# MLP down products of layers 1 and 2 in plain fp32, and the key and value projections of the last layer folded into other weights

## The chip, the cores and the metric

The kernel runs on one core of a Trainium2 chip. The metric is the device time of one execution in microseconds. The time before is the median of three runs.

## What is computed

Four different transformer layers run one after the other on x of 64 batches x 128 tokens x 128 channels, with a condition vector and a context of 77 tokens per batch. Layer 0 has windowed attention, top-k cross attention and a SwiGLU MLP; layers 1 and 2 have self attention, cross attention and a GELU MLP; the last one mixes the context in and routes each token over three experts. The change touches the GELU MLP of layers 1 and 2 and the last layer:

```python
# layers 1 and 2, MLP (512 hidden channels)
x_norm2 = modulate(_ln(x), shift_m, scale_m)
h = gelu(x_norm2 @ W_mlp1 + b_mlp1)
x = x + gate_m[:, None] * (h @ W_mlp2 + b_mlp2)
# last layer
nx = layer_norm(x, gamma, beta)
q = nx @ Wq;  k = context @ Wk;  v = context @ Wv
weights = softmax(q @ k.T * H ** -0.5)
evidence = weights @ v
combined = concatenate([nx, evidence, anchor], axis=-1)
router_probs = softmax(combined @ router_W + router_b)
h = silu(combined @ e_w1 + e_b1)          # three experts, 256 hidden channels each
routed = sum((h @ e_w2 + e_b2) * router_probs)
g = sigmoid(silu(combined @ gate_w1 + gate_b1) @ gate_w2 + gate_b2)
x + g * (routed @ out_w + out_b)
```

## The kernel before

x stays in SBUF from the first load to the last store (`x_res`). Each stage is a block with a list of instructions per engine, written by hand, and the engines are tied by counting semaphores; a list is worked through in order, and the stages follow each other with a barrier. All stages work on groups of G = 4 batches, 16 groups, so that a matmul has 4 x 128 = 512 columns, one PSUM bank.

A product in the MLPs and for the up products of the last layer is made of three fp32r matmuls (`product3`, L236 to L240): weights and input are each split into a high part (a cast to fp32r) and a low part (the value minus the high part), and low x high, high x low and high x high are summed in PSUM. Other products are plain fp32 matmuls.

`mlp_phase` (L1775) is used for three layers. For layers 1 and 2 (`swiglu` false) a group runs so: DVE takes the statistics of x (`ln_stats`, `ln_variance`), POOL takes the power -0.5 (`rstd_of`), DVE normalises (`ln_apply`, L1895), PE transposes (L2008), ACT modulates into `hT`, DVE splits `hT` in two (`split_h`, L1902 and L1904). Then for each of NC = 4 chunks of 128 hidden channels: PE makes the up product into one of four banks `u_ps`; ACT applies GELU into `hid` (L1993); DVE casts the high part (L1943); POOL subtracts for the low part (L1870), in the fourth chunk DVE does (L1949); PE makes the down product into `y_ps`, LD = 3 chunks behind the up product. ACT then applies the gate (`apply_gate`, L1970), PE transposes back (L2048), and DVE adds to x (L1924). The lists work on neighbouring groups at once: in the body of group g, PE transposes `xn` of group g + 1 after the first chunk and `pg` of group g - 2 in the second, DVE has x of g - 2, the statistics of g + 2 and `split_h` of g + 1 in its list. PE's list of the down product waits for the low part:

```python
pe.wait_ge(s_lo, n + 1)
product3(nc, y_ps[:, par, :], parts(w2, c * C), [hid2[:, c, k, :] for k in range(2)],
         start=(c == 0), stop=(c == NC - 1)).then_inc(s_down, 1)
```

`refine_phase` (L2057) is the last layer. For iteration i its PE list has the seven up products of group i (`up`, two banks `u_ps`, each product six fp32r matmuls: three on the normalised x, three on the evidence), and between them the small steps of groups i + 1 and i + 2: transposed attention weights and evidence of i + 1 (L2511, L2518), transposes of `xn` of i + 2 (L2481), the router of i + 1 (L2528, L2530), then key, query and value projections of i + 2 (L2486, L2491, L2496) through one bank `l_ps`, and the scores (L2503); at its end the gate (L2581) and the down products of i (L2593). The three projections follow each other through `l_ps`: ACT copies the keys out, then the queries, and DVE the values, and the next projection waits for the copy before. ACT evacuates each up product with four SiLU (L2420). Before group 0, `prepare` multiplies weights with each other (e2 with the output matrix, the anchor parts) once the weights have landed, and ACT and POOL split the up weights `w1s`.

## Time and profile before

| | us |
|---|---|
| median of three runs | 3493.57 |
| lowest, highest run | 3489.97, 3500.9 |
| profiled execution, its time | 3496.01 |
| profiled execution, its span | 3494.2 |
| PE busy | 3048.8 (87%) |
| PE weight loads | 2051.7 (59%) |
| DVE busy | 2754.6 (79%) |
| ACT busy | 2253.2 (64%) |
| POOL busy | 1170.7 (34%) |
| mean granted TensorE clock | 0.947 |

The span is the time from the first to the last instruction of the profiled execution; its time also has what lies around that. Busy shares are means over stages with different limits. In the order of the program: layer 0's attentions end near 1240 us; its MLP follows until about 1430; layer 1's attentions until 2097, its MLP until 2247; layer 2's attentions until 2934, its MLP until 3084; then the last layer to the end. A duration of a matmul is longer than the distance to the next one, as matmuls overlap; lengths are best read from start to start. The granted clock is 1.00 at 2.4 GHz and 0.50 at 1.2 GHz.

### The profile page before, as it was taken

The numbers are of one execution on the slowest core, as the hardware profiler recorded it, in microseconds if no ns is written. First come the engines' busy times: TensorE is split into PE (matmuls) and PEld (weight loads), VectorE is DVE, ScalarE is ACT, GpSimd is POOL, SyncE is SP. The second block draws the span as 40 slices with busy tenths as digits, with TensorE's granted clock in tenths as the row PEclk, the third lists the DMA queues.
The fourth block names the chain that finished last, engine by engine and source line by source line (L and its number), as shares of the span: only waits on it lengthen the run. The fifth ranks groups of instructions, "written<-read, shape, count | busy, mean of one in ns | idle before, by whom it ended". The sixth has DMA issues, their size and how long they took to land. (4 is left out here: it accounts for less than half of the span.)

```text
span 3494.2 us, 94730 instructions
## 1 busy us (share of the span) xinstructions
PE 3048.8 (87%) x32127; PEld 2051.7 (59%) x32127; DVE 2754.6 (79%) x12477; ACT 2253.2 (64%) x5572; POOL 1170.7 (34%) x1374
## 2 busy tenths in 40 slices
PE   6999967777777779799999997789999997879999
PEld 3444434444444457566666665556666665568887
DVE  4878779999999978588877759778887776946665
ACT  2666667777777667377766665457776665646665
POOL 0000046666666656311122215521112212532111
PEclk9999979999899889799999999989999999979999
DMA  1111000000000000244444420034444440000000
GB/s 47 44 49 37 14 12 7 9 9 9 8 9 7 3 1 1 72 106 107 107 103 100 104 60 1 20 97 108 106 107 101 105 100 17 1 24 13 11 12 16
DMA packets 139908, 162.90 MB, mean 47 GB/s; under 512 B 41318, under 2 KB 88870, under 8 KB 139174
## 3 DMA queue, kind: packets, MB, share of 16 engines
q1 hardware_dynamic: 127270, 130.80, 14.9%
q0 software_dynamic: 12160, 26.04, 3.2%
q8 instruction: 262, 4.29, 0.5%
q14 instruction: 216, 1.77, 0.2%
HBM read 16.33 MB, written 4.19 MB: 6 GB/s over the span
## 5 line engine op out<-in xcount | busy, mean ns | idle before, releaser
L1374 ACT ACTIVATE attn_pT<-attn_t 128x512 f32<-128x512 f32 (+1 forms) x1024 | 555.7, 597 | 319.7 <-PE attn_t L1631 319.5
L1491 DVE TENSOR_REDUCE attn_mx<-attn_s 128x4 f32<-128x512 f32 (+1 forms) x1024 | 549.4, 578 | 140.2 <-PE attn_s L1616 139.1
L1616 PEld LDWEIGHTS attn_s<-packed_keys,packed_queries 32*128 32x128 f32 x4096 | 276.7, 189 | 161.5 <-DVE attn_mx L1491 96.0
L659 ACT ACTIVATE topk_prob<-topk_s,topk_nmx 128x77 f32<-128x77 f32 x1024 | 248.3, 326 | 181.7 <-DVE topk_work L840 156.0
L1289 POOL DMA_DIRECT2D packed_queries<-attn_om x256 | 142.7, 557 | 645.0 <-ACT attn_om L1367 640.9
L1616 PE MATMUL attn_s<-packed_keys,packed_queries 32*128 32x128 f32 (+1 forms) x4096 | 341.5, 287 | 13.3 <-DVE attn_mx L1491 7.2
L503 POOL TENSOR_SCALAR topk_mask<-topk_work 128x308 f32<-128x308 f32 x256 | 250.1, 977 | 238.9 <-DVE topk_work L845 237.8
L1023 PE MATMUL topk_s<-kbd,topk_qT 128*128 128x308 f32 x512 | 215.4, 505 | 129.7 <-ACT topk_prob L659 129.2
L1656 PE MATMUL attn_o<-attn_pT,attn_vp 128*18 128x128 f32 (+1 forms) x8192 | 326.3, 277 | 0.0
L1631 PE MATMUL attn_t<-packed_queries,packed_keys 32*128 32x128 f32 (+1 forms) x4096 | 299.8, 264 | 0.0
L1870 POOL TENSOR_TENSOR mlp_hid<-mlp_hid 128x512 fp32r<-128x512 f32 x160 | 210.1, 1314 | 156.8 <-DVE mlp_hid L1943 107.9
L1631 PEld LDWEIGHTS attn_t<-packed_queries,packed_keys 32*128 32x128 f32 (+1 forms) x4096 | 227.4, 166 | 4.7 <-ACT attn_pT L1374 3.4
L1676 PE MATMUL attn_l<-packed_keys 128*128 128x512 f32 x636 | 225.2, 444 | 0.7 <-DVE attn_vp L1481 0.7
L507 POOL TENSOR_TENSOR topk_prob<-topk_prob,topk_mask 128x308 f32<-128x308 f32 x256 | 213.8, 835 | 21.3
L840 DVE MATCH_REPLACE8 topk_work<-topk_top,topk_s 128x77 f32<-128x77 f32 x1024 | 220.2, 223 | 0.0
L1656 PEld LDWEIGHTS attn_o<-attn_pT,attn_vp 128*18 128x18 f32 (+1 forms) x8192 | 181.3, 97 | 60.6 <-issue 44.4
L845 DVE MATCH_REPLACE8 topk_work<-topk_top,topk_work 128x77 f32<-128x77 f32 x1024 | 215.3, 219 | 0.0
L1023 PEld LDWEIGHTS topk_s<-kbd,topk_qT 128*128 128x128 f32 x512 | 86.6, 210 | 195.5 <-ACT topk_prob L659 141.4
L1033 PEld LDWEIGHTS topk_t<-ident,topk_prob 128*77 128x77 f32 x1024 | 146.5, 163 | 58.2 <-issue 16.5
L829 DVE MAX8 topk_top<-topk_s 128x8 f32<-128x77 f32 x1024 | 167.0, 222 | 15.4 <-PE topk_s L1023 15.0
L1033 PE MATMUL topk_t<-ident,topk_prob 128*77 128x128 f32 x1024 | 170.4, 294 | 1.8 <-POOL topk_prob L507 1.8
L1285 POOL TENSOR_TENSOR attn_rstd<-attn_vareps,neg_half 128x4 f32<-128x4 f32 x64 | 65.8, 1029 | 299.9 <-DVE attn_vareps L1449 299.8
(316 smaller groups left out, 7869.7 us busy)
## 6 DMA issues: line engine op xcount, KB each, us to landing
packed_queries<-attn_qT SPq DMA_DIRECT2D x720, 64.0 KB, 2.2
packed_keys<-attn_kT SPq DMA_DIRECT2D x384, 64.0 KB, 2.1
packed_queries<-attn_om POOLq DMA_DIRECT2D x256, 64.0 KB, 2.3
packed_queries<-zero_rows SPq DMA_DIRECT2D x120, 128.0 KB, 2.7
packed_keys<-attn_kT SPq DMA_DIRECT2D x384, 39.0 KB, 2.2
kbd<-window_kT SPq DMA_DIRECT2D x512, 8.0 KB
kbd<-topk_kT SPq DMA_DIRECT2D x512, 4.8 KB
x_res<-in_x SPq DMA_DIRECT2D x16, 192.0 KB, 2.6
```

Source lines behind the costliest of these rows:

```text
L503: nc.gpsimd.tensor_scalar(mask[:, u % 2, :], work[:, n % NP, :], NEG / 2, None, ALU.is_le).then_inc(s_mask, 1)
L659: last = nc.scalar.activation(prob[:, n % NP, h * keys:(h + 1) * keys], s_ps[:, u % 2, h * keys:(h + 1) * keys], ACT.Exp, scale=SCALE, bia ...
L840: last = nc.vector.match_replace(wk_[now][:, h, :], top[:, u % 2, h, :], sc[:, h, :], NEG)
L845: last = nc.vector.match_replace(wk_[past][:, h, :], top2[:, c % 2, h, :], wk_[past][:, h, :], NEG)
L1023: last = nc.tensor.matmul(s_ps[:, u % 2, 0:cols], qT[:, par, b * T:(b + 1) * T], r.kbd[:, HU * g:HU * g + HU, b * keys:(b + 1) * keys], st ...
L1033: last = nc.tensor.transpose(t_ps[0:rows, c % 2, j * T:(j + 1) * T], prob[:, n % NP, j * rows:(j + 1) * rows], r.ident[:, :])
L1374: nc.scalar.activation(pT[0:keys, c % 2, h, :], t_ps[0:keys, h, :], ACT.Exp, scale=SCALE).then_inc(s_exp, 1)
L1491: nc.vector.tensor_reduce(mx[:, (c // 2) % 2, 2 * k + h, :], sc, AX.X, ALU.max).then_inc(s_max, 1)
L1616: last = nc.tensor.matmul(s_ps[:, h, k * KW:(k + 1) * KW], r.qp[32 * j:32 * j + 32, buf, k, b * T:(b + 1) * T], r.kp[32 * j:32 * j + 32, b ...
L1631: last = nc.tensor.matmul(t_ps[0:keys, h, k * T:(k + 1) * T], r.kp[32 * j:32 * j + 32, buf, k, b * KW:b * KW + keys], r.qp[32 * j:32 * j + ...
L1656: last = nc.tensor.matmul(o_ps[32 * k:32 * k + 18, v * T:(v + 1) * T], vp[0:keys, buf, b, k, v, a, :], pT[0:keys, c % 2, a, k * T:(k + 1) ...
L1676: nc.tensor.matmul(l_ps[:, :], r.kp[:, buf, 0, 0:T], r.kp[:, buf, 0, :], start=True, stop=True)
```

## The change

In the MLP of layers 1 and 2, the hidden values and the down weights are no longer split. A down product is one fp32 matmul of `hid` with the weights as they lie in SBUF; it waits for GELU alone, and GELU waits for the down product that read the same buffer. DVE's cast and DVE's or POOL's subtraction go, and the split of the down weights ahead of the first group. Layer 0's MLP stays as it is, with three fp32r matmuls.

In the last layer the host hands over Wq, Wk and Wv transposed. The kernel multiplies Wq by the transpose of Wk once (`wqk`), projects the queries with that, and takes the scores against the raw context. The evidence becomes the weights' mean of the raw context, which is loaded by DMA from SP's queue, four batches a time, into three buffers; Wv is multiplied once into the parts of the expert, gate and router weights that the evidence meets (`folded`, `wr`), in `prepare`. ACT takes the high parts of these from PSUM, DVE the low parts. The key and value projections of every group go, with ACT's copy of the keys and DVE's copy of the values.

```diff
-        w1, w2 = sb("w1", [C, 2, W1], F32R), sb("w2", [C, 2, NC * C], F32R)
+
+        w1 = sb("w1", [C, 2, W1], F32R)
+        w2 = sb("w2", [C, 2, NC * C], F32R) if swiglu else None
...
-                    if swiglu or c < NC - 1:
+                    if swiglu:
...
-                split_weights(nc, nc.vector.tensor_copy, dve, w2, r.W(name, 0, NC * C), s_w, 2)
+                if swiglu:
+                    split_weights(nc, nc.vector.tensor_copy, dve, w2, r.W(name, 0, NC * C), s_w, 2)
...
-                    if not swiglu:
-                        after(dve, s_down, n - 3)
-                        dve.wait_ge(s_hid, n + 1)
-                        nc.vector.tensor_copy(hid2[:, c, 0, :], hid[:, c % NB, :]).then_inc(s_hi, 1)
                     if c == 2 and nxt2:
                         ln_apply(g + 2)
-                    if c == 3 and not swiglu:
-                        dve.wait_ge(s_hi, n + 1)
-                        after(dve, s_lo, n)
-                        nc.vector.tensor_tensor(hid2[:, c, 1, :], hid[:, c % NB, :], hid2[:, c, 0, :].bitcast(F32),
-                                                ALU.subtract).then_inc(s_lo, 1)
...
-                        after(act, s_lo, n - 3)
+                        after(act, s_down, n - 3)
...
-                    pe.wait_ge(s_w, 4)
+                    if swiglu:
+                        pe.wait_ge(s_w, 4)
+                if not swiglu:
+                    pe.wait_ge(s_hid, n + 1)
+                    nc.tensor.matmul(y_ps[:, par, :], r.W(name, c * C), hid[:, c % NB, :],
+                                     start=(c == 0), stop=(c == NC - 1)).then_inc(s_down, 1)
+                    return
                 pe.wait_ge(s_lo, n + 1)
                 product3(nc, y_ps[:, par, :], parts(w2, c * C), [hid2[:, c, k, :] for k in range(2)],
                          start=(c == 0), stop=(c == NC - 1)).then_inc(s_down, 1)
...
-        qT, kT, v = sb("qT", [C, GT]), sb("kT", [C, K4]), sb("v", [S, G, C])
+        qT, v = sb("qT", [C, GT]), sb("v", [S, 3, G, C])
...
+        def folded():
+
+            yield t_ps[:, :].rearrange("c (e n) -> c e n", e=2), [up_part(p, 1)[:, 0:2] for p in range(2)]
+            yield u_ps[:, 1:2, 2 * C:2 * C + RH], [up_part(p, 1)[:, 2:3] for p in range(2)]
+            yield g_ps[:, B * E:B * E + C], [w1s[:, p, E * 2 * RH + C:NU] for p in range(2)]
...
+            def load_values(g):
+                sp.dma_start(v[:, g % 3], r.ctx_v[:, G * g:G * g + G, :]).then_inc(s_vin[g % 3], 16)
...
+            for g in range(3):
+                load_values(g)
             for g in range(NG):
                 p = g % 2
+                if there(g + 3):
+                    sp.wait_ge(s_eps, g + 1)
+                    load_values(g + 3)
...
-                nc.gpsimd.tensor_tensor(w1s[:, 1, 0:E * 2 * RH].rearrange("c (e n) -> c e n", e=E), e1_parts,
-                                        w1s[:, 0, 0:E * 2 * RH].bitcast(F32).rearrange("c (e n) -> c e n", e=E),
-                                        ALU.subtract).then_inc(s_w1lo, 1)
-                nc.gpsimd.tensor_tensor(w1s[:, 1, E * 2 * RH:NU], r.W("g1", 0, 2 * C),
-                                        w1s[:, 0, E * 2 * RH:NU].bitcast(F32), ALU.subtract).then_inc(s_w1lo, 1)
+                nc.gpsimd.tensor_tensor(up_part(1, 0), e1_first, up_part(0, 0).bitcast(F32), ALU.subtract
+                                        ).then_inc(s_w1lo, 1)
+                nc.gpsimd.tensor_tensor(w1s[:, 1, E * 2 * RH:E * 2 * RH + C], r.W("g1", 0, C),
+                                        w1s[:, 0, E * 2 * RH:E * 2 * RH + C].bitcast(F32), ALU.subtract
+                                        ).then_inc(s_w1lo, 1)
...
-            def values_out(g):
-                dve.wait_ge(s_vps, g + 1)
-                nc.vector.tensor_copy(v[:, :, :], l_ps[0:S, :].rearrange("p (b c) -> p b c", b=G)
-                                      ).then_inc(s_v, 1)
...
+                for k, (product, parts) in enumerate(folded()):
+                    dve.wait_ge(s_fhi, k + 1)
+                    nc.vector.tensor_tensor(parts[1], product, parts[0].bitcast(F32), ALU.subtract).then_inc(s_flo, 1)
...
-            def keys_out(g):
-                act.wait_ge(s_kps, g + 1)
-                nc.scalar.copy(kT[:, :], l_ps[:, 0:K4]).then_inc(s_kT, 1)
...
+                for k, (product, parts) in enumerate(folded()):
+                    if k == 2:
+                        act.wait_ge(s_arb, 1)
+                        nc.scalar.copy(wr[:, :], g_ps[:, B * E + C:B * E + C + E]).then_inc(s_wr, 1)
+                    nc.scalar.copy(parts[0], product).then_inc(s_fhi, 1)
+
+            act.wait_ge(s_qkps, 1)
+            nc.scalar.copy(wqk[:, :], t_ps[:, 0:C]).then_inc(s_wqk, 1)
...
-                after(pe, s_v, g)
+                after(pe, s_qT, g)
                 pe.wait_ge(s_xn, g + 1)
                 for b in range(G):
                     last = nc.tensor.transpose(l_ps[:, b * T:(b + 1) * T], xn[:, b, :], r.ident[:, :])
                 last.then_inc(s_xT, 1)
 
-            def project_keys(g):
+            def project_queries(g):
                 pe.wait_ge(s_nx, g + 1)
-                nc.tensor.matmul(l_ps[:, 0:K4], r.W("k3"), r.ctxT[:, G * g:G * g + G, :], start=True, stop=True
-                                 ).then_inc(s_kps, 1)
-
-            def project_queries(g):
-                pe.wait_ge(s_kT, g + 1)
-                nc.tensor.matmul(l_ps[:, :], r.W("q3"), nx[:, g % NXB, :], start=True, stop=True).then_inc(s_qps, 1)
-
-            def project_values(g):
+                if g == 0:
+                    pe.wait_ge(s_wqk, 1)
+                nc.tensor.matmul(l_ps[:, :], wqk[:, :], nx[:, g % NXB, :], start=True, stop=True).then_inc(s_qps, 1)
+
+            def scores(g):
+                after(pe, s_dif, g)
                 pe.wait_ge(s_qT, g + 1)
                 for b in range(G):
-                    last = nc.tensor.matmul(l_ps[0:S, b * C:(b + 1) * C], r.ctxT[:, G * g + b, :], r.W("v3"),
-                                            start=True, stop=True)
-                last.then_inc(s_vps, 1)
-
-            def scores(g):
-                after(pe, s_dif, g)
-                for b in range(G):
                     last = nc.tensor.matmul(s_ps[:, b * S:(b + 1) * S], qT[:, b * T:(b + 1) * T],
-                                            kT[:, b * S:(b + 1) * S], start=True, stop=True)
+                                            r.ctxT[:, G * g + b, :], start=True, stop=True)
...
-                pe.wait_ge(s_v, g + 1)
+                pe.wait_ge(s_vin[g % 3], 16 * (g // 3) + 16)
                 pe.wait_ge(s_pT, g + 1)
                 for b in range(G):
-                    last = nc.tensor.matmul(t_ps[:, b * T:(b + 1) * T], v[:, b, :], pT[:, b * T:(b + 1) * T],
+                    last = nc.tensor.matmul(t_ps[:, b * T:(b + 1) * T], v[:, g % 3, b, :], pT[:, b * T:(b + 1) * T],
                                             start=True, stop=True)
...
-                                            r.W("rw", E, E), start=False, stop=True)
+                                            wr[:, :], start=False, stop=True)
...
+                pe.wait_ge(s_wqk, 1)
+                for e in range(E):
+                    out = t_ps[:, e * RH:(e + 1) * RH] if e < 2 else u_ps[:, 1, 2 * C:2 * C + RH]
+                    nc.tensor.matmul(out, r.W("v3"), r.W("e1", (e * 3 + 1) * RH, RH), start=True, stop=True)
+                nc.tensor.matmul(g_ps[:, B * E:B * E + C], r.W("v3"), r.W("g1", C), start=True, stop=True)
+                nc.tensor.matmul(g_ps[:, B * E + C:B * E + C + E], r.W("v3"), r.W("rw", E, E), start=True, stop=True)
                 for k in range(2 * E):
...
+            nc.tensor.matmul(t_ps[:, 0:C], r.W("q3"), r.W("k3"), start=True, stop=True).then_inc(s_qkps, 1)
...
-        "q3": a(L3 + "Wq"), "k3": a(L3 + "Wk"), "v3": a(L3 + "Wv"), "rw": rows(a(L3 + "router_W")),
+        "q3": a(L3 + "Wq").T, "k3": a(L3 + "Wk").T, "v3": a(L3 + "Wv").T, "rw": rows(a(L3 + "router_W")),
```

What this does to the lists. On DVE in an MLP of layer 1 or 2, one group's worth before (`mlp_hid` is the hidden tile, `mlp_hT` the modulated input, `mlp_xn` the normalised x):

```order
L1949 TENSOR_TENSOR mlp_hid<-mlp_hid 128x512
L1879 BN_STATS mlp_stats<-x_res 128x6 x4
L1943 CAST mlp_hid<-mlp_hid 128x512
L1924 TENSOR_TENSOR x_res<-mlp_r,x_res 128x512
L1886 BN_AGGR mlp_mv<-mlp_stats 128x2 x4
L1889 TENSOR_SCALAR mlp_vareps<-mlp_mv 128x4
L1943 CAST mlp_hid<-mlp_hid 128x512
L1902 CAST mlp_hT<-mlp_hT 128x512
L1904 TENSOR_TENSOR mlp_hT<-mlp_hT 128x512
L1943 CAST mlp_hid<-mlp_hid 128x512
L1895 TENSOR_SCALAR mlp_xn<-x_res,mlp_mv,mlp_rstd 128x128 x4
```

and of the change:

```order
L1881 BN_STATS mlp_stats<-x_res 128x6 x4
L1927 TENSOR_TENSOR x_res<-mlp_r,x_res 128x512
L1888 BN_AGGR mlp_mv<-mlp_stats 128x2 x4
L1891 TENSOR_SCALAR mlp_vareps<-mlp_mv 128x4
L1904 CAST mlp_hT<-mlp_hT 128x512
L1906 TENSOR_TENSOR mlp_hT<-mlp_hT 128x512
L1897 TENSOR_SCALAR mlp_xn<-x_res,mlp_mv,mlp_rstd 128x128 x4
```

The four casts of `mlp_hid` and its subtraction are gone from between the others, which keep their order.

On PE in the same stage, from the down product before the transposes of `xn` to the next but one, before:

```order
L238 MATMUL mlp_y<-mlp_hid,mlp_w 128x512
L239 MATMUL mlp_y<-mlp_hid,mlp_w 128x512
L240 MATMUL mlp_y<-mlp_hid,mlp_w 128x512
L2008 MATMUL mlp_l<-ident,mlp_xn 128x128 x4
L238 MATMUL mlp_u<-mlp_hT,mlp_w 128x512
L239 MATMUL mlp_u<-mlp_hT,mlp_w 128x512
L240 MATMUL mlp_u<-mlp_hT,mlp_w 128x512
L238 MATMUL mlp_y<-mlp_hid,mlp_w 128x512
L239 MATMUL mlp_y<-mlp_hid,mlp_w 128x512
L240 MATMUL mlp_y<-mlp_hid,mlp_w 128x512
L2048 MATMUL mlp_r<-ident,mlp_pg 128x128 x4
```

and of the change, where L2002 is the L2008 of before:

```order
L2029 MATMUL mlp_y<-mlp_hid,weights 128x512
L2002 MATMUL mlp_l<-ident,mlp_xn 128x128 x4
L238 MATMUL mlp_u<-mlp_hT,mlp_w 128x512
L239 MATMUL mlp_u<-mlp_hT,mlp_w 128x512
L240 MATMUL mlp_u<-mlp_hT,mlp_w 128x512
L2029 MATMUL mlp_y<-mlp_hid,weights 128x512
L2048 MATMUL mlp_r<-ident,mlp_pg 128x128 x4
```

Each three matmuls into `mlp_y` have become one that reads `mlp_hid` and the resident weights.

On PE in the last layer, from the end of the router of group i + 1 to the scores of i + 2, before (six matmuls into `refine_u` are one up product):

```order
L2530 MATMUL refine_g<-weights,refine_ev 128x3
L2486 MATMUL refine_l<-ctxT,weights 128x308
L238 MATMUL refine_u<-refine_nxs,refine_w1s 128x512
...
L240 MATMUL refine_u<-refine_evs,refine_w1s 128x512
L2491 MATMUL refine_l<-refine_nx,weights 128x512
L238 MATMUL refine_u<-refine_nxs,refine_w1s 128x512
...
L240 MATMUL refine_u<-refine_evs,refine_w1s 128x512
L2496 MATMUL refine_l<-weights,ctxT 77x128 x4
L238 MATMUL refine_u<-refine_nxs,refine_w1s 128x512
...
L240 MATMUL refine_u<-refine_evs,refine_w1s 128x512
L2503 MATMUL refine_s<-refine_kT,refine_qT 128x77 x4
```

and of the change:

```order
L2544 MATMUL refine_g<-refine_wr,refine_ev 128x3
L238 MATMUL refine_u<-refine_nxs,refine_w1s 128x512
...
L240 MATMUL refine_u<-refine_evs,refine_w1s 128x512
L2507 MATMUL refine_l<-refine_nx,refine_wqk 128x512
L238 MATMUL refine_u<-refine_nxs,refine_w1s 128x512
...
L240 MATMUL refine_u<-refine_evs,refine_w1s 128x512
L238 MATMUL refine_u<-refine_nxs,refine_w1s 128x512
...
L240 MATMUL refine_u<-refine_evs,refine_w1s 128x512
L2513 MATMUL refine_s<-ctxT,refine_qT 128x77 x4
```

The keys (L2486) and values (L2496) are gone, the queries have moved from L2491 to L2507 with `refine_wqk`, and the scores read `ctxT`.

## Rows read from the trace of the kernel before

**Rows 1.** The core's span and granted clock.

```profile
core 0: 3494.2 us, clock 0.947
```

**Rows 2.** Windows: us, busy PE PEld DVE ACT POOL, clock, DMA share, GB/s.

```profile
2112.40:2238.00 125.60, 103.26 (x466) 74.04 (x465) 115.25 (x290) 79.75 (x172) 72.99 (x58) 1.00 0.00 1
...
3128.80:3437.00 308.20, 307.22 (x2005) 268.06 (x2006) 194.70 (x594) 191.99 (x515) 65.21 (x53) 1.00 0.05 12
```

**Rows 3.** Timeline, MLP of layer 1: start, us, engine, line, operation [idle before].

```profile
2114.11 0.47 PE L238 MATMUL mlp_u<-mlp_hT,mlp_w 128*128 128x512 f32 x1 [0.85 <-ACT mlp_hid L1993]
...
2124.86 0.63 PE L2008 MATMUL mlp_l<-ident,mlp_xn 128*128 128x128 f32 x4 [1.40 <-DVE mlp_xn L1895]
...
2228.61 0.63 PE L2008 MATMUL mlp_l<-ident,mlp_xn 128*128 128x128 f32 x4 [1.41 <-DVE mlp_xn L1895]
```

**Rows 4.** Timeline, the same stage, POOL and DVE side by side.

```profile
2138.37 1.37 POOL L1870 TENSOR_TENSOR mlp_hid<-mlp_hid 128x512 fp32r<-128x512 f32 x1
...
2138.51 1.52 DVE L1943 CAST mlp_hid<-mlp_hid 128x512 fp32r<-128x512 f32 x1
```

**Rows 5.** Timeline, PE in one group of layer 1's MLP.

```profile
2177.90 0.39 PE L238 MATMUL mlp_y<-mlp_hid,mlp_w 128*128 128x512 f32 x1
...
2178.60 0.60 PE L2048 MATMUL mlp_r<-ident,mlp_pg 128*128 128x128 f32 x4
...
2179.27 0.40 PE L239 MATMUL mlp_u<-mlp_hT,mlp_w 128*128 128x512 f32 x1
```

**Rows 6.** Timeline, DVE in the same group.

```profile
2179.24 0.69 DVE L1924 TENSOR_TENSOR x_res<-mlp_r,x_res 128x512 f32<-128x512 f32 x1 [0.48 <-PE mlp_r L2048]
...
2180.33 0.43 DVE L1943 CAST mlp_hid<-mlp_hid 128x512 fp32r<-128x512 f32 x1
...
2181.13 0.69 DVE L1904 TENSOR_TENSOR mlp_hT<-mlp_hT 128x512 fp32r<-128x512 f32 x1
```

**Rows 7.** Timeline, PE in layer 0's MLP.

```profile
1336.01 0.39 PE L240 MATMUL mlp_y<-mlp_hid,mlp_w 128*128 128x512 f32 x1
...
1337.40 0.39 PE L239 MATMUL mlp_u<-mlp_hT,mlp_w 128*128 128x512 f32 x1
```

**Rows 8.** Timeline, PE in the refine stage, one group.

```profile
3298.26 0.77 PE L2486 MATMUL refine_l<-ctxT,weights 128*128 128x308 f32 x2
...
3299.33 0.39 PE L240 MATMUL refine_u<-refine_nxs,refine_w1s 128*128 128x512 f32 x1
...
3300.26 1.02 PE L2491 MATMUL refine_l<-refine_nx,weights 128*128 128x512 f32 x2
...
3301.59 0.39 PE L240 MATMUL refine_u<-refine_nxs,refine_w1s 128*128 128x512 f32 x1
...
3302.51 1.03 PE L2496 MATMUL refine_l<-weights,ctxT 128*77 128x128 f32 x8
...
3303.86 0.40 PE L240 MATMUL refine_u<-refine_nxs,refine_w1s 128*128 128x512 f32 x1
...
3321.20 0.77 PE L2486 MATMUL refine_l<-ctxT,weights 128*128 128x308 f32 x2
```

**Rows 9.** Timeline, PE at the start of the refine stage.

```profile
3091.12 1.39 PE L2486 MATMUL refine_l<-ctxT,weights 128*128 128x308 f32 x2 [0.87 <-ACT refine_nx L2380]
3093.02 2.08 PE L2491 MATMUL refine_l<-refine_nx,weights 128*128 128x512 f32 x2 [0.50 <-ACT refine_kT L2385]
3095.77 1.99 PE L2496 MATMUL refine_l<-weights,ctxT 128*77 128x128 f32 x8 [0.68 <-ACT refine_qT L2389]
3097.55 1.83 PE L2503 MATMUL refine_s<-refine_kT,refine_qT 128*128 128x77 f32 x8
3099.18 2.74 PE L2538 MATMUL refine_e<-condT,refine_weights 128*128 128x64 f32 x12
...
3117.83 1.38 PE L2486 MATMUL refine_l<-ctxT,weights 128*128 128x308 f32 x2
...
3125.81 0.77 PE L238 MATMUL refine_u<-refine_nxs,refine_w1s 128*128 128x512 f32 x1
```

More of the change, by code:

```diff
@@ L1808, in mlp_phase @@
         hid = sb("hid", [C, NB, GT])
-        hid2 = sb("hid2", [C, NC, 2, GT], F32R)
+        hid2 = sb("hid2", [C, NC, 2, GT], F32R) if swiglu else None
         pg = sb("pg", [C, GT])
@@ L2081, in refine_phase @@
         w2ow = sb("w2ow", [C, 2 * E, C])
+        wqk, wr = sb("wqk", [C, C]), sb("wr", [C, E])
         b2bc, b2t = sb("b2bc", [C, E, C]), sb("b2t", [T, E, C])
@@ L2117, in refine_phase @@
         s_stats, s_mv, s_var, s_rstd, s_xn = sem("stats"), sem("mv"), sem("var"), sem("rstd"), sem("xn")
-        s_xT, s_nx, s_kps, s_kT, s_qps, s_qT, s_vps, s_v = (
-            sem(n) for n in ("xT", "nx", "kps", "kT", "qps", "qT", "vps", "v"))
+        s_xT, s_nx, s_qps, s_qT = (sem(n) for n in ("xT", "nx", "qps", "qT"))
+        s_vin = [sem("vin0"), sem("vin1"), sem("vin2")]
+        s_qkps, s_wqk, s_fhi, s_flo, s_wr = (sem(n) for n in ("qkps", "wqk", "fhi", "flo", "wr"))
         s_nxhi, s_nxlo, s_evhi, s_evlo = sem("nxhi"), sem("nxlo"), sem("evhi"), sem("evlo")
@@ L2140, in spread, with up_part @@
             return ap.rearrange("p (b a) -> p b a", a=1).broadcast_to([T, G, n])
-        e1_parts = r.W("e1", 0, E * 3 * RH).rearrange("c (e n) -> c e n", e=E)[:, :, 0:2 * RH]
+        e1_first = r.W("e1", 0, E * 3 * RH).rearrange("c (e n) -> c e n", e=E)[:, :, 0:RH]
+        def up_part(p, half):
+            return w1s[:, p, 0:E * 2 * RH].rearrange("c (e n) -> c e n", e=E)[:, :, half * RH:half * RH + RH]
+        def folded():
+            yield t_ps[:, :].rearrange("c (e n) -> c e n", e=2), [up_part(p, 1)[:, 0:2] for p in range(2)]
+            yield u_ps[:, 1:2, 2 * C:2 * C + RH], [up_part(p, 1)[:, 2:3] for p in range(2)]
+            yield g_ps[:, B * E:B * E + C], [w1s[:, p, E * 2 * RH + C:NU] for p in range(2)]
         @block.sync
         def _(sp):
+            def load_values(g):
+                sp.dma_start(v[:, g % 3], r.ctx_v[:, G * g:G * g + G, :]).then_inc(s_vin[g % 3], 16)
             sp.dma_start(r.w3[:, :], io["weights3"]).then_inc(s_w3, 16)
@@ L2355, in _ @@
                 if there(i + 2):
-                    values_out(i + 2)
                     difference(i + 2)
@@ L2426, in prepare @@
                 act.wait_ge(s_w3, 16)
-                if split:
-                    nc.scalar.copy(w1s[:, 0, 0:E * 2 * RH].rearrange("c (e n) -> c e n", e=E), e1_parts
-                                   ).then_inc(s_w1hi, 1)
-                    nc.scalar.copy(w1s[:, 0, E * 2 * RH:NU], r.W("g1", 0, 2 * C)).then_inc(s_w1hi, 1)
+                nc.scalar.copy(up_part(0, 0), e1_first).then_inc(s_w1hi, 1)
+                nc.scalar.copy(w1s[:, 0, E * 2 * RH:E * 2 * RH + C], r.W("g1", 0, C)).then_inc(s_w1hi, 1)
             def prepared():
@@ L2455, in _ @@
                     hidden(i, 3)
-                if new:
-                    keys_out(i + 2)
                 if now:
@@ L2508, in transpose_weights @@
                 after(pe, s_ev, g)
+                if g == 0:
+                    pe.wait_ge(s_flo, 1)
                 pe.wait_ge(s_pn, g + 1)
@@ L2524, in router @@
                     pe.wait_ge(s_arb, 1)
+                    pe.wait_ge(s_wr, 1)
+                    pe.wait_ge(s_flo, 3)
                 after(pe, s_tg, g - 1)
@@ L2557, in up @@
                         pe.wait_ge(s_w1lo, 2)
+                        pe.wait_ge(s_flo, 3)
                 after(pe, s_hid, n - 1)
@@ L2614, in _ @@
                     router(i + 1)
-                if new:
-                    project_keys(i + 2)
                 if now:
@@ L2622, in _ @@
                     up(i, 5)
-                if new:
-                    project_values(i + 2)
                 if now:
```

## The prediction

> **What bounds the kernel now.** I first read the core's span and clock, then a table of the stages by windows, then the timeline inside the two stages that the change touches. The profiled execution has a span of 3494.2 us [rows 1] and took 3496.0 us; the median of the three runs is 3493.57, so 2.4 us come off at the end.
>
> In the MLP of layer 1, from 2112.4 to 2238.0, PE is busy for 103.3 of 125.6 us, DVE for 115.3, ACT for 79.8 and POOL for 73.0; a layer 2 group repeats it. PE isn't full there. Each group begins with four transposes that wait 1.40 us for `xn` from DVE, and those at 2124.86 and 2228.61 are 12 groups apart: 8.65 us a group [rows 3]. DVE's own list sets that time. It holds four casts of `hid` and one subtraction; one that meets POOL's subtraction of 1.37 us takes 1.52 [rows 4], one alone 0.43, and the subtraction on DVE has the width of L1904, 0.69 us [rows 6].
>
> The refine stage is the other case: from 3128.8 to 3437.0 PE is busy for 307.2 of 308.2 us at clock 1.00, DVE and ACT for less than two thirds [rows 2]. A group takes 22.94 us, from the key projection at 3298.26 to the next at 3321.20 [rows 8]. There every matmul removed is worth its own length.
>
> **MLP down products, layers 1 and 2.** Per chunk the change takes away DVE's cast, the subtraction on POOL or DVE, and three fp32r matmuls, and puts one fp32 matmul in. *PE's list per group.* Three fp32r matmuls run from 2177.90 to 2178.60, 0.70 us or 0.233 each; a set of four transposes costs 2178.60 to 2179.27 less one such matmul, 0.43 us [rows 5]. One fp32 matmul 128x512 stands in the refine stage: from 3300.26 to 3301.59 lie it and two fp32r matmuls, so it costs 1.33 - 0.47 = 0.86 us [rows 8]. PE's list before is then 8 x 0.70 + 2 x 0.43 = 6.46 us, and after it 4 x 0.70 + 4 x 0.86 + 0.86 = 7.10. PE gets 0.64 us more work per group, 20 us in all over 32 groups; that alone is no loss as long as the group stays under 8.65.
>
> The Trainium skill, "FP8 and Floating Point Precision", TensorE Precision Notes, says that true FP32 takes four passes through the array, and "TensorE: Matmul & The Clock Gate", "Wait — 56ns, not 53.3ns?", gives 215.7 ns for a warm pass of 512 columns. By these two pages of the Trainium skill (an estimate) a product goes from 0.65 to 0.86 us, a larger step than by the rows, and the list after comes to 6.9 us. The one pass is 0.233 here and not 0.216, so I keep the rows.
>
> *DVE's list* falls from 7.9 us a group (115.3 of 125.6 us [rows 2], times 8.65) by 3 x 0.43 + 1.52 + 0.69 = 3.50, to 4.4. ACT's is unchanged, 79.8 / 125.6 x 8.65 = 5.5 us. POOL keeps one small power instruction a group. So PE has the longest list.
>
> *Does a chain bind before the lists do?* PE transposes `pg` in chunk 1; DVE then adds to x, finishes the variance, splits `hT` and lets PE begin the next group. In one group the transposes start at 2178.60 [rows 5], the add at 2179.24, 0.64 us later, and the last subtraction ends at 2181.82. Of these 2.58 us a cast of `hid` at 2180.33 goes away, so 2.2 remain [rows 6]. From the group's start to those transposes PE needs 2 x 1.56 + 0.43 = 3.55 us. Together 3.55 + 0.64 + 2.2 + 0.1 for the handover = 6.5, 0.6 under PE's list. It's near, but it doesn't bind.
>
> *What PE-bound groups really take.* Layer 0's MLP keeps PE full with the same skeleton. From 1336.01 to 1337.40 there lie a set of the first transposes and two fp32r matmuls: 1.39 - 0.47 = 0.92 us for a set that costs 0.43 in layer 1 [rows 5, 7]. So a group without slack pays up to 0.49 us more at its start. Fewer instructions stand in PE's queue after the change, so I take half: 7.10 + 0.25 = 7.35 us, with 7.10 and 7.6 as ends.
>
> *Sum per layer.* 13 steady steps x (8.65 - 7.35) = 16.9 us. In the first group PE waits 0.85 us at 2114.11, on work that DVE did beside POOL [rows 3], and 0.8 us of its next wait; both go: 1.5. The last two groups are PE's own work and gain about 0.2. In the prologue the split of the down weights goes from DVE, but hides behind POOL's power instruction and ACT's modulation; I cost it at nothing, and if that cover weren't there it would be 1.1 us a layer. Per layer 18.6, for two **37.2 us** (ends 31 and 44).
>
> **Refine stage, steady groups.** Three edits go together. The key projection: 3298.26 to 3299.33 holds it and two fp32r matmuls, 1.07 - 0.47 = 0.60 us; some 0.08 of that is the change from fp32 to fp32r, which stays, as the router's small matmuls are now in front, so 0.52. The value projection: 3302.51 to 3303.86 holds it and two, 0.88 us, and goes whole, as two up products now meet [rows 8]. The query projection stays with other weights. 1.40 us a group, and the 14 groups i = 0 to 13 issue these for group i + 2: **19.6 us** (ends 16 and 21). ACT loses one evacuation and DVE another, on engines with slack; I cost them at nothing. The raw context now comes by DMA on SP's queue, 77 x 4 x 128 x 4 bytes = 158 KB a group in three buffers. It is asked for when the group three before has had its evidence, some two groups, 46 us, ahead, and the stores behind that wait want a later event, so I cost it at nothing; from PE's side it could only hurt if a load took longer than that.
>
> **Refine stage, start.** The stage starts at half clock: four value products of 128 columns take 1.78 us (3095.77 to 3097.55) [rows 9], twice the 0.88 us at full clock [rows 8]. Keys, values and their evacuations go twice from a chain on which PE waits. Group 0: scores begin at 3097.55 now; queries began at 3093.02 and could begin at the keys' place, 3091.12, and values go, so scores are 1.9 + 1.8 = 3.7 us earlier and `prepare` can start at 3095.5 instead of 3099.18. It then has five more products: at half clock 0.44 us per 128 columns, 7 x 0.44 plus a small one = 3.2 us. So it ends 0.5 earlier. Behind it DVE has three more subtractions of up to 512 columns, 1.4 us by the 0.69 of such an instruction [rows 6], ahead of softmax(0). Net 0.9 us late there. Group 1: keys begin at 3117.83 and the first up product at 3125.81, 8.0 us; without keys and values, queries, one evacuation and scores remain, 4.4 us. So the first up product comes 3.6 - 0.9 = 2.7 us earlier [rows 9]. Some of it is lost if the clock rises no earlier, so **1.9 us** (ends 0 and 5).
>
> **Sum.** 37.2 + 19.6 + 1.9 = 58.7 us. 3496.0 - 58.7 = 3437.3 for a run like the profiled one, and 2.4 less for the median: **3435 us**. With all ends together it is 3424 to 3447.
>
> **The rivals.** A difference under 0.3%, 10.5 us, counts as no change.
> 1. The chain over DVE binds the MLP. For: only 0.6 us of slack, and its handovers come in a row. Against: no POOL work of 512 columns is left to stretch a DVE instruction. At 8.1 us a group it saves 0.55 x 26 = 14 instead of 34: 3455 us. Chance 0.12.
> 2. ACT's seven evacuations of u, with two banks, pace PE in the refine stage. For: queries, up 5 and up 6 now follow closely. Against: ACT is busy for 192 of 308 us [rows 2]. With half of the 19.6 us kept: 3445 us. Chance 0.10.
> 3. The lean case: no handover cost, group 7.1, a good start. 3435 - 26 x 0.25 - 2 = 3426 us. The Trainium skill's 215.7 ns for a pass, cited above, speaks for it. Chance 0.15.
> 4. Slower. PE, now dense with fp32, is granted half clock in the MLPs. A group would take some 14.2 us, 5.6 more than before. The saving is gone once 58.7 / 6.9 = 9 of the 26 groups run so; a whole layer at half clock gives 3435 + 13 x 6.9 = 3525 us. Against: the granted clock is 1.00 in the MLP and in the refine stage, which is full with both kinds of matmul [rows 2]. Chance 0.02.
> 5. The change doesn't do what it says (the queue order around it, or a load late): about 3490. Chance 0.02.
>
> **How the numbers follow.** My forecast as worked out has 0.59, the rivals the rest. The range has to hold the time 8 times in 10: 3420 to 3452 takes in my ends, rivals 2 and 3, and stops short of rivals 1, 4 and 5 (0.16). Faster 0.96, within 0.3% 0.02, slower 0.02.
>
> **What would show it.** In the MLPs: the first transposes no longer wait for DVE, groups 7.1 to 7.6 us apart, DVE near 4.4 us a group; the fp32 down product 0.86 us from start to start. In refine: groups 21.5 us apart, PE still full, the first up product 2.7 us earlier against the stage's start than at 3125.81. I am wrong if PE still waits for `xn` or `hT` more than 0.3 us a group, if an fp32 product costs over 1.24 us (then PE's list reaches 8.65), if PE has gaps before up products in refine, or if any steady stretch shows a clock under 1.

## The result, and the profile after

The change makes the kernel faster: 3437.5 us (median of 4 runs, 3430.2 to 3441.1) against 3493.2 for the kernel before, ratio 0.9835 (0.9812 to 0.9858). The forecast was 3435, with a range of 3420 to 3452. Two later jobs timed the same kernel at 3426.0 and 3429.9, ratios 0.9813 (0.9793 to 0.9833) and 0.9812 (0.9796 to 0.9827), so the first comparison lies a little high, though the intervals overlap. Its profiled execution is also its longest, 3441.1 us. The table of stages says where the time went. A stage is counted up to the start of DVE's last addition to x; "start" is from there to the first up product of the last layer.

| us | layer 0 and layer 1's attentions | MLP 1 | attentions 2 | MLP 2 | start | rest | span |
|---|---|---|---|---|---|---|---|
| before | 2096.2 | 150.2 | 686.9 | 150.2 | 42.3 | 368.4 | 3494.2 |
| after, first comparison | 2100.1 | 127.8 | 697.7 | 127.8 | 37.5 | 348.6 | 3439.3 |
| after, second job | 2097.0 | 128.3 | 688.1 | 128.0 | 36.3 | 348.7 | 3426.3 |

The four touched stages gave 22.4 + 22.4 + 4.8 + 19.8 = 69.4 us. Some 14.7 of them were lost in stages that the change doesn't touch: 10.8 in the attentions of layer 2, 3.9 before layer 1's MLP. The page of after:

```profile
span 3439.3 us, 93774 instructions
```

```profile
PE 3029.5 (88%) x31851; PEld 2015.6 (59%) x31851; DVE 2612.0 (76%) x12300; ACT 2246.9 (65%) x5561; POOL 1041.2 (30%) x1278
```

The windows view of after over 12 groups of layer 1's MLP and over the steady part of the last layer, with the columns of [rows 2]:

```profile
2125.13:2210.01 84.88, 84.88 (x337) 54.68 (x336) 48.10 (x188) 66.46 (x145) 13.43 (x12) 1.00 0.00 1
...
3120.00:3390.00 270.00, 270.00 (x1751) 235.59 (x1750) 172.48 (x536) 172.31 (x468) 62.78 (x51) 1.00 0.08 21
```

In both PE is busy the whole time at clock 1.00. PE in the MLP was busy for 103.3 of 125.6 us before [rows 2]; DVE now works 48.1 / 12 = 4.0 us a group.

The timeline of after in layer 1's MLP, the counterpart of [rows 3] and [rows 6]:

```profile
2125.13 0.60 PE L2002 MATMUL mlp_l<-ident,mlp_xn 128*128 128x128 f32 x4
...
2155.42 0.60 PE L2048 MATMUL mlp_r<-ident,mlp_pg 128*128 128x128 f32 x4
...
2156.06 0.69 DVE L1927 TENSOR_TENSOR x_res<-mlp_r,x_res 128x512 f32<-128x512 f32 x1 [2.69 <-PE mlp_r L2048]
2156.55 1.02 PE L2029 MATMUL mlp_y<-mlp_hid,weights 128*128 128x512 f32 x2
2157.32 1.12 POOL L1844 TENSOR_TENSOR mlp_rstd<-mlp_vareps,neg_half 128x4 f32<-128x4 f32 x1 [5.96 <-DVE mlp_vareps L1891]
2157.87 0.39 PE L240 MATMUL mlp_u<-mlp_hT,mlp_w 128*128 128x512 f32 x1
2158.54 1.12 DVE L1897 TENSOR_SCALAR mlp_xn<-x_res,mlp_mv,mlp_rstd 128x128 f32<-128x128 f32 x4 [0.24 <-POOL mlp_rstd L1844]
...
2160.50 0.60 PE L2002 MATMUL mlp_l<-ident,mlp_xn 128*128 128x128 f32 x4
...
2210.01 0.60 PE L2002 MATMUL mlp_l<-ident,mlp_xn 128*128 128x128 f32 x4
```

The first transposes no longer wait. 2125.13 and 2210.01 are 12 groups apart: 7.07 us a group, against 8.65. Between 2156.55 and 2157.87 lie one fp32 product and two fp32r matmuls: 1.32 - 0.47 = 0.85 us. `xn` is complete at 2159.66 and wanted at 2160.50, so 0.84 us of slack is left.

In the last layer the query projection marks a group ([rows 8] had the keys):

```profile
3276.37 1.02 PE L2507 MATMUL refine_l<-refine_nx,refine_wqk 128*128 128x512 f32 x2
...
3297.88 1.02 PE L2507 MATMUL refine_l<-refine_nx,refine_wqk 128*128 128x512 f32 x2
```

21.51 us, where it was 22.94. And its start, for [rows 9], with the first DMA issue of the stage:

```profile
3054.71 0.37 SPq L2164 DMA_DIRECT2D refine_weights<-in_weights  x1
...
3063.61 1.99 PE L2513 MATMUL refine_s<-ctxT,refine_qT 128*128 128x77 f32 x8 [0.68 <-ACT refine_qT L2405]
...
3068.75 2.00 PE L2558 MATMUL refine_e<-condT,refine_weights 128*128 128x64 f32 x12
...
3078.14 1.11 PE L2523 MATMUL refine_t<-ident,refine_pn 128*77 128x128 f32 x4 [4.58 <-DVE refine_pn L2281]
...
3090.74 0.77 PE L238 MATMUL refine_u<-refine_nxs,refine_w1s 128*128 128x512 f32 x1
```

The first up product comes 36.03 us after that DMA issue. Before, with the issue at 3084.98, it came after 40.83.

### The profile page after: what moved, and what is told of

Same layout as the page of the kernel before. It is cut to its first block and busy times, and to the rows that moved or that the text cites. A ratio compares the mean times of both kernels' runs of the same rounds, so it can differ in the third digit from the quotient of the medians.

```text
span 3439.3 us, 93774 instructions
## 1 busy us (share of the span) xinstructions
PE 3029.5 (88%) x31851; PEld 2015.6 (59%) x31851; DVE 2612.0 (76%) x12300; ACT 2246.9 (65%) x5561; POOL 1041.2 (30%) x1278
## 5 line engine op out<-in xcount | busy, mean ns | idle before, releaser
L834 DVE MAX8 topk_top<-topk_work 128x8 f32<-128x77 f32 x1024 | 163.4, 218 | 0.0
L1285 POOL TENSOR_TENSOR attn_rstd<-attn_vareps,neg_half 128x4 f32<-128x4 f32 x64 | 65.8, 1028 | 318.0 <-DVE attn_vareps L1449 318.0
## 6 DMA issues: line engine op xcount, KB each, us to landing
packed_queries<-zero_rows SPq DMA_DIRECT2D x120, 128.0 KB, 2.7
```

## The experiments

Four jobs, each with the kernel before beside it (medians 3491.7, 3492.5 and 3495.6 us in the three later ones).

**The halves alone, and both kernels again.** e1 is the kernel before with the MLP hunks of the diff, e2 with the last layer's hunks; e3 and e10 are the changed kernel, e4 is the kernel before.

> The MLP edit alone, the last layer as before. Theory (PE-bound groups): groups of 7.07 us in both MLPs as in the changed kernel's trace, 22.5 us less per layer, 45 us in the stages; the time then depends on whether the layer 2 attention is longer again. If the attention's extra 11 us comes from the MLP edit, the time falls by 45 - 11 - 4 = 30 us to 3463; if it was chance of one execution, by 45 us to 3448.

> The fold in the last layer alone, MLPs as before (8.65 us a group). Theory: 19.9 us in the steady groups and 4.8 at the start of the last layer, 25 us less: 3468. Rival: the gain at the start hung on the state of PE's clock after the changed MLP and falls to 2, giving 3471. The layer 2 attention should stay at 691 us if the MLP edit is what lengthened it, and anywhere from 691 to 703 if it is chance.

> The changed kernel once more. If the 10.8 us by which the layer 2 attention was longer is a lasting cost of the change, the second profile shows 702 to 704 us there too; if it is chance of one execution, 691 to 698. The touched stages should repeat within 1 us, the start of the last layer too if the early rise of the clock there is no accident.

> The kernel before once more, one look. If the attention stages vary by chance, layer 2's is not 691.8 us again but some us off; if it is a lasting cost of the change, it is 691 to 693 again.

| | us (lowest, highest, runs) | ratio (interval) | MLP 1, MLP 2 | start | rest |
|---|---|---|---|---|---|
| e1 | 3446.5 (3445.0, 3450.6, 4) | 0.9875 (0.9859 to 0.9890) | 128.0, 128.1 | 42.1 | 368.4 |
| e2 | 3464.8 (3461.1, 3468.0, 4) | 0.9925 (0.9909 to 0.9941) | 150.2, 150.2 | 36.5 | 348.3 |
| e3 | 3426.0 (3422.6, 3431.0, 4) | 0.9813 (0.9793 to 0.9833) | 128.3, 128.0 | 36.3 | 348.7 |
| e4 | 3495.8 (one run) | | 150.2, 149.9 | 43.2 | 367.7 |

By the medians, 45.2 us for e1 and 27.0 for e2 make 72.2, which is 6.4 more than the 65.8 of e3. In the touched stages the parts do add up: 44.6 us for e1 and 25.9 for e2 make 70.5, against 69.9 for e3. So they don't help or hurt each other there, and the 6.4 us lie in the stages that no edit touches. e1's start is that of the kernel before (42.1 for 42.3), so the faster start belongs to the last layer's edit alone. The attentions of layer 2, where these four have the same code, took 683.8, 677.6, 688.1 and 684.4 us, a spread about as large as the loss in the first comparison. (The expectations count this stage 4.9 us longer, up to the next MLP's first transposes: their 691.8 is the table's 686.9. So e3, at 693.0 by that count, didn't repeat the 702.6 of the first comparison.) The windows view of that stage in after and in e2:

```profile
2227.77:2925.47 697.70, 644.03 (x9768) 435.60 (x9768) 517.69 (x1730) 446.15 (x900) 133.87 (x208) 0.96 0.39 95
```

```profile
2249.10:2926.65 677.55, 632.73 (x9768) 429.05 (x9768) 517.71 (x1729) 447.20 (x900) 133.84 (x208) 0.98 0.40 98
```

The same instructions; PE's busy time and its granted clock differ (0.96 and 0.98), and 8.9 us more are idle.

**What set 8.65 us a group?** In theory DVE's list; the rivals were PE's handover and POOL. e5 keeps PE's short way but does all the old split work, unread:

```diff
+        hid2 = sb("hid2", [C, NC, 2, GT], F32R)
...
+                    if swiglu or c < NC - 1:
                         pool.wait_ge(s_hi, n + 1)
...
+                    if not swiglu:
+                        after(dve, s_lo, n - 3)
+                        dve.wait_ge(s_hid, n + 1)
+                        nc.vector.tensor_copy(hid2[:, c, 0, :], hid[:, c % NB, :]).then_inc(s_hi, 1)
```

with DVE's subtraction in the fourth chunk and ACT's wait for `s_lo` back as well. e6 keeps only POOL's part of it:

```diff
+                    elif c < NC - 1:
+                        pool.wait_ge(s_hid, n + 1)
+                        nc.gpsimd.tensor_tensor(hid2[:, c, 1, :], hid[:, c % NB, :], r.W(name, 0, GT),
+                                                ALU.subtract).then_inc(s_lo, 1)
...
+                        if c < NC - 1:
+                            after(act, s_lo, 3 * (g - 1) + c + 1)
```

and e11 only DVE's four casts:

```diff
+                    if not swiglu:
+                        dve.wait_ge(s_hid, n + 1)
+                        nc.vector.tensor_copy(hid2[:, c, 0, :], hid[:, c % NB, :]).then_inc(s_hi, 1)
...
+                        after(act, s_hi, n - 3)
```

> The changed kernel, but DVE's casts of hid and the subtractions on POOL and DVE stay in their lists; nothing reads what they write, and GELU waits for them before it overwrites hid. So PE has the short way and DVE the long list. Theory (DVE's list set the 8.65 us, not PE's three matmuls or the wait for the low part): groups of 8.5 to 8.8 us again, each MLP 150 us from the last add of the attention to its own. Rival (the wait of the down product for POOL's low part set it): 7.1 to 7.4 us a group, 128 to 133 us.

> The changed kernel with one subtraction of 512 columns on POOL in chunks 0 to 2 of every group, which nothing reads, and no cast on DVE. DVE's list is 4.4 us, POOL's 3.9 and 1.0. Theory: PE's list of 7.07 us still binds, the MLPs stay at 128 us. Rival (my chain over DVE, put at 6.5 us, binds once a DVE instruction in it is stretched by POOL, as the cast was by 1.1 us): 7.6 to 7.9 us a group, 136 to 140 us.

> The changed kernel with DVE's four casts of hid a group kept, which nothing reads, and no subtraction on POOL or DVE. DVE's list is 4.4 + 1.7 = 6.1 us. Theory (lock-outs by POOL, not DVE's own instructions, made the 8.65 us): no cast is stretched, groups stay at 7.07 to 7.2 us and each MLP at 128 to 130 us, where POOL's subtractions alone (e6) gave groups of 9.2 and more. Rival (DVE's list as such was the bound and its waits add to it): 7.6 to 8.2 us, 136 to 145 us.

One run each, read from the stages. The MLPs took 152.1 and 152.2 us in e5 (3475.1 in all), 164.1 and 162.4 in e6 (3488.9), 128.0 and 128.2 in e11 (3437.2). In e5 the long group is back, 8.79 us, though PE makes one matmul of each down product and waits for no low part, so neither of these set it. In e11 a group is 7.09 us: the casts, 1.7 us a group by their lengths, cost nothing. POOL's three subtractions cost 35 us a layer though no instruction reads their result. Timelines of e6 and e11:

```profile
2145.19 0.63 PE L2008 MATMUL mlp_l<-ident,mlp_xn 128*128 128x128 f32 x4 [1.95 <-DVE mlp_xn L1901]
...
2149.11 1.12 POOL L1844 TENSOR_TENSOR mlp_rstd<-mlp_vareps,neg_half 128x4 f32<-128x4 f32 x1 [4.41 <-DVE mlp_vareps L1895]
...
2150.20 3.73 POOL L1876 TENSOR_TENSOR mlp_hid<-mlp_hid,weights 128x512 fp32r<-128x512 f32 x3
2150.34 3.93 DVE L1901 TENSOR_SCALAR mlp_xn<-x_res,mlp_mv,mlp_rstd 128x128 f32<-128x128 f32 x4 [0.24 <-POOL mlp_rstd L1844]
...
2154.41 0.63 PE L2008 MATMUL mlp_l<-ident,mlp_xn 128*128 128x128 f32 x4 [1.96 <-DVE mlp_xn L1901]
```

```profile
2126.05 0.60 PE L2006 MATMUL mlp_l<-ident,mlp_xn 128*128 128x128 f32 x4
...
2145.34 0.42 DVE L1945 CAST mlp_hid<-mlp_hid 128x512 fp32r<-128x512 f32 x1
2145.68 1.11 DVE L1897 TENSOR_SCALAR mlp_xn<-x_res,mlp_mv,mlp_rstd 128x128 f32<-128x128 f32 x4
...
2211.09 0.60 PE L2006 MATMUL mlp_l<-ident,mlp_xn 128*128 128x128 f32 x4
```

In e6 POOL's subtractions stand right behind its power instruction. They start 0.14 us ahead of DVE's `ln_apply`, which needs that power, and the four instructions of `ln_apply` take 3.93 us instead of 1.11. PE then waits 1.96 us for `xn`; this group takes 9.22 us with DVE's list at its shortest. One by one, POOL's three end at 2151.48, 2152.71 and 2153.93, and the first three instructions of `ln_apply` at 2151.57, 2152.79 and 2154.01; the fourth, which meets none, takes 0.33. (Of the 15 steps from group to group in layer 1, four took 10.7 to 10.9 us at a mean granted clock of 0.84, the steady others 9.2 at 1.00. That is 6.4 of the 36 us over the changed kernel's MLP, so not all of its 164 us are the stretched instruction.) With this in hand the kernel before reads otherwise. Its timeline, one group:

```profile
2176.74 0.63 PE L2008 MATMUL mlp_l<-ident,mlp_xn 128*128 128x128 f32 x4 [1.40 <-DVE mlp_xn L1895]
...
2180.50 1.12 POOL L1842 TENSOR_TENSOR mlp_rstd<-mlp_vareps,neg_half 128x4 f32<-128x4 f32 x1 [0.36 <-DVE mlp_vareps L1889]
...
2181.59 1.37 POOL L1870 TENSOR_TENSOR mlp_hid<-mlp_hid 128x512 fp32r<-128x512 f32 x1
2181.74 1.51 DVE L1943 CAST mlp_hid<-mlp_hid 128x512 fp32r<-128x512 f32 x1
...
2183.16 2.06 DVE L1895 TENSOR_SCALAR mlp_xn<-x_res,mlp_mv,mlp_rstd 128x128 f32<-128x128 f32 x4
...
2185.38 0.63 PE L2008 MATMUL mlp_l<-ident,mlp_xn 128*128 128x128 f32 x4 [1.40 <-DVE mlp_xn L1895]
```

From L2008 to L2048 are 1.86 us, in which PE is full (2176.74 in these lines to 2178.60 [rows 5]). The add to x starts 0.64 us later, at 2179.24 [rows 6]. From there DVE works through its list without a gap (none over 0.04 us) to the end of `ln_apply` at 2185.22, 5.98 us, and the next L2008 starts 0.16 us after that: 8.64, the whole group, with no slack on the way. All 12 steady groups have these 5.98 to 6.00 us. This loop, from PE over DVE's add, variance, split, casts and `ln_apply` back to the transposes, was what bound the stage. POOL's power isn't on it here: it ends at 2181.62, when DVE still has `split_h` and a cast before it. In e6, where no cast stands there, `ln_apply` does wait for it. Two DVE steps on the loop are stretched by POOL, by 1.51 - 0.43 = 1.1 and 2.06 - 1.11 = 0.95 us; without them the loop would be 6.6 us, under PE's list. e5 fits as well: its first part is 0.15 us longer, since an fp32 product stands before the second transposes, and so is its group, 8.79.

The Trainium skill, "SBUF — State Buffer", SBUF: two separate sides, says that VectorE and GpSimd share a port pair by an exclusive lock, which whoever starts first holds for its whole instruction; on VectorE's side it names instructions in a two-port mode, or with two inputs in SBUF. The trace agrees: 3.93 us beside 3.73 us of POOL, and 1.11 without; in e6 each held instruction ends 0.08 us after POOL's.

**Split two chunks out of four.** If that is the mechanism, the place of POOL's work decides, not its amount. e7 keeps the split for chunks 0 and 2, e9 for chunks 0 and 3; the other two are plain fp32:

```diff
+        SPLIT = (0, 1, 2, 3) if swiglu else (0, 2)
...
+                    if c in SPLIT:
+                        pool.wait_ge(s_hi, nth(g, c) + 1)
...
+                    if not swiglu and c in SPLIT:
+                        after(dve, s_down, n - 3)
+                        dve.wait_ge(s_hid, n + 1)
+                        nc.vector.tensor_copy(hid2[:, c, 0, :], hid[:, c % NB, :]).then_inc(s_hi, 1)
...
-                if not swiglu:
+                if c not in SPLIT:
                     pe.wait_ge(s_hid, n + 1)
```

with `(0, 3)` in e9.

> The changed kernel with chunks 0 and 2 of each group split again (cast on DVE, subtraction on POOL, three fp32r matmuls), chunks 1 and 3 plain fp32, down weights split in the prologue. PE's list falls by 2 x 0.16 to 6.75 us, DVE's is 4.4 + 0.9 plus what POOL stretches, the chain over DVE 6.5. Theory: groups of 6.75 to 6.8 us, MLPs 123.5 us, 9 us less than the changed kernel. Rival (the chain or the stretched cast binds): 7.1 to 7.6 us a group, no gain or a loss of up to 14 us.

> The changed kernel with chunks 0 and 3 split (three fp32r matmuls), 1 and 2 plain. Theory after e6 and e7: what binds is the normalisation of the next group but one, when POOL has a subtraction of 512 columns queued behind its power instruction and locks DVE out; with chunks 0 and 3 POOL's subtractions fall beside the add to x and beside the statistics, which were not stretched. Groups of 6.75 to 6.8 us, each MLP 4.5 us shorter than the changed kernel's 128, 9 us in all. Rival (any two split chunks cost the chain as much as in e7, 7.44 us a group): MLPs of 132 us and more.

> The changed kernel beside e9, for a comparison in one job: 65 to 70 us under the kernel before by the sum of the touched stages (44.6 in the MLPs, 19.8 in the steady groups of the last layer, 5 to 6.5 at its start); the first comparison's 56 us would be repeated only if the layer 2 attention's extra time were lasting.

| | us (lowest, highest, runs) | ratio (interval) | MLP 1, MLP 2 |
|---|---|---|---|
| e7 | 3435.0 (3427.8, 3436.8, 4) | 0.9825 (0.9807 to 0.9843) | 132.1, 132.3 |
| e9 | 3416.5 (3413.2, 3425.9, 4) | 0.9781 (0.9762 to 0.9800) | 123.4, 123.4 |
| e10 | 3429.9 (3426.9, 3433.3, 5) | 0.9812 (0.9796 to 0.9827) | 128.0, 128.1 |

e7 and e9 both have two subtractions a group on POOL and a shorter list on PE than the changed kernel. Timelines of e7 and e9:

```profile
2151.01 0.63 PE L2010 MATMUL mlp_l<-ident,mlp_xn 128*128 128x128 f32 x4 [0.47 <-DVE mlp_xn L1902]
...
2156.17 1.28 POOL L1877 TENSOR_TENSOR mlp_hid<-mlp_hid 128x512 fp32r<-128x512 f32 x1
2156.24 2.06 DVE L1902 TENSOR_SCALAR mlp_xn<-x_res,mlp_mv,mlp_rstd 128x128 f32<-128x128 f32 x4
...
2158.45 0.63 PE L2010 MATMUL mlp_l<-ident,mlp_xn 128*128 128x128 f32 x4 [0.46 <-DVE mlp_xn L1902]
```

```profile
2145.15 0.60 PE L2010 MATMUL mlp_l<-ident,mlp_xn 128*128 128x128 f32 x4
...
2150.27 1.12 DVE L1902 TENSOR_SCALAR mlp_xn<-x_res,mlp_mv,mlp_rstd 128x128 f32<-128x128 f32 x4 [0.24 <-POOL mlp_rstd L1849]
...
2151.64 0.87 DVE L1886 BATCH_NORM_STATS2 mlp_stats<-x_res 128x6 f32<-128x128 f32 x4
2151.81 1.28 POOL L1877 TENSOR_TENSOR mlp_hid<-mlp_hid 128x512 fp32r<-128x512 f32 x1 [1.64 <-DVE mlp_hid L1950]
2151.93 0.60 PE L2010 MATMUL mlp_l<-ident,mlp_xn 128*128 128x128 f32 x4
```

In e7 one subtraction meets `ln_apply` (2.06 us), PE waits, and a group takes 7.44 us: two products are faster, and the stage is slower. In e9 none meets it (1.12 us), PE waits for nothing, and a group takes 6.78. The two kernels differ only in which of chunks 2 and 3 is split, and that is 17.6 us over both MLPs. e9 beats both kernels: 13.3 us under e10 in the same job, of which the MLPs explain 9.3.

**Keys alone.** e8 is e1 with the keys folded (`wqk`, scores on `ctxT`), the values as before:

```diff
-                pe.wait_ge(s_kT, g + 1)
-                nc.tensor.matmul(l_ps[:, :], r.W("q3"), nx[:, g % NXB, :], start=True, stop=True).then_inc(s_qps, 1)
+                pe.wait_ge(s_nx, g + 1)
+                if g == 0:
+                    pe.wait_ge(s_wqk, 1)
+                nc.tensor.matmul(l_ps[:, :], wqk[:, :], nx[:, g % NXB, :], start=True, stop=True).then_inc(s_qps, 1)
```

> MLP edit, and of the fold only Wk into Wq: the key projection and ACT's copy go, the value projection, DVE's copy and the expert weights stay as before. Theory: steady groups lose 0.52 us of 22.94 (22.42), the stage from the first up product to the end 368.4 - 14 x 0.52 = 361; the start is some 3.5 us shorter than 42, as queries take the keys' place twice. Rival (the key term is 0.60, nothing remains of it): 22.34 and 360.

One run, 3448.9 us. The rest took 361.1 us: 368.4 - 361.1 = 7.3 = 14 x 0.52 for the keys, and 361.1 - 348.7 (e3) = 12.4 = 14 x 0.89 for the values. The start took 39.2, between e1's 42.1 and e3's 36.3; that is 2.9 us off e1's, where 3.5 were expected.

## Why the prediction was right, and where it wasn't

The forecast was a gain of 58.7 us. The first comparison showed 55.7 between the medians, the repeats 65.8 and 65.7, which the range still holds. The close hit was luck in part: the touched stages gave 69 to 70, some 11 more than forecast, and in the first comparison the untouched ones took 14.7 back.

*PE's list.* Right: 7.10 us a group by the rows, 7.07 measured; 0.86 for an fp32 product, 0.85 measured. The 6.9 us from the Trainium skill's 215.7 ns a pass was further off.

*"DVE's own list sets that time."* This step failed. The list was 7.9 us long beside a group of 8.65, and I took the remaining 0.75 for nothing. e11 has a DVE list with all four casts and loses nothing; e6 has the shortest list and is the slowest. The bound was the loop over `xn`: 1.86 us of PE, 0.64 and 0.16 for the handovers, and 5.98 of DVE's list, of which 2.0 are instructions held by POOL. I had counted the stretched cast and not `ln_apply`, which is one reason why DVE's list came to 4.0 us and not to 4.4. The forecast of this stage was still near, since the change removes POOL's subtractions too, and PE's list was next either way.

*"Does a chain bind before the lists do?"* I walked the chain over `hT` (6.5 us) and missed the one over `xn`, which in the changed kernel goes over POOL's power (`ln_apply` waits 0.24 us for it). It takes 1.99 us from L2002 at 2153.43 to L2048 at 2155.42 and 4.24 from there to the end of `ln_apply`, 6.2 in all. That it doesn't bind was right, with 0.84 us of slack. Rival 1 stays away in the changed kernel; e5, e6 and e7 bring it back.

*7.10 + 0.25 for the handover.* Failed: it cost nothing. Layer 0's 0.49 [rows 7] doesn't carry over. This term, 13 x 0.25 = 3.3 us a layer, is most of what 22.4 exceeds my 18.6 by. Rival 3's group length was the right one.

*Refine, steady.* Right: 1.43 us a group and 19.8 in all for 1.40 and 19.6. PE stays full, so rival 2 is out, and the added DMA costs nothing visible there. e8 confirms both terms apart, 0.52 and 0.89 for 0.52 and 0.88.

*Refine, start.* Under-sized: 4.8 us in the first comparison and about 6 in e2 and e3 for 1.9 (my end was 5). The scores did come 3.7 us earlier, 8.9 us after the first DMA issue instead of 12.6. But `prepare` ended 2.5 us earlier, where I had 0.5. Its five added products took 3.4 us for my 3.2; the old ones behind them took 4.85 us instead of 7.21, and I had left those as they were, at half clock. The windows view of both kernels over the scores and `prepare`:

```profile
3095.00:3106.30 11.30, 10.62 (x51) 10.16 (x50) 2.72 (x7) 4.00 (x5) 4.91 (x3) 0.55 0.01 1
```

```profile
3064.70:3073.50 8.80, 8.80 (x49) 7.90 (x48) 2.32 (x7) 1.53 (x4) 3.96 (x4) 0.71 0.00 1
```

The granted clock is 0.55 before and 0.71 after, and the same twelve matmuls took 2.74 us before [rows 9], 2.00 after and 1.53 in e2. The clock first goes to 1.00 at 15.0 us after the stage's first DMA issue in after, and at 20.2 before. All nine profiles of kernels with the whole fold have it at 12.5 to 15.0 us; before, e1 and e8 have it at 19.8 to 20.2, and e4 only at 42.9. Where it comes at 14.7 to 15.0 (after, e5, e6, e7) the first up product follows the issue by 35.9 to 36.0 us, in the other five by 34.8 to 35.1: that is the difference between 4.8 and 6.

What brings it back earlier stays open. PE was busy without a gap in the second view and idle for 0.7 us in the first, but gaps alone aren't it. In e8 and in e10 PE waits alike, 0.87 us for `nx` and 0.7 for `qT`, and from 8.9 us after the issue it has no gap to the end of `prepare`. The windows from there, e8 and then e10:

```profile
3057.23:3068.00 10.77, 10.77 (x49) 10.54 (x50) 3.01 (x8) 3.37 (x4) 6.14 (x4) 0.50 0.01 2
```

```profile
3057.03:3066.00 8.97, 8.96 (x52) 8.08 (x52) 2.31 (x7) 2.64 (x4) 4.98 (x5) 0.77 0.08 24
```

e8 stays at half clock throughout, e10 doesn't; what differs is which matmuls run. DVE's three subtractions cost 0.68 + 0.41 + 0.28 = 1.37 us, as forecast, and group 1 gave 3.5 for my 3.6.

*Rivals 4 and 5* didn't come: the clock is 1.00 in both MLP and refine windows.

**Open.** Why the attentions of layer 2 take 677.6 to 697.7 us with the same code isn't settled. Kernels whose MLP has four plain products and no subtraction on POOL (after, e1, e3, e8, e10, e11) had 683.8 to 697.7 there, mean 692.1; the others (before, e2, e4, e5, e6, e7, e9) 677.6 to 688.6, mean 685.4. That hints at a few us given back behind an MLP that keeps PE full with fp32, but the two sets overlap and no run isolates it. The stage's granted clock goes with it over all 13 profiles: 0.96 in the five of after, e3, e8, e10 and e11 (688.0 to 697.7 us), 0.97 to 0.98 in the other eight (677.6 to 688.6). What sets that clock, no run shows. It isn't in the forecast and isn't explained.
